# Query, output and transpose matmuls reordered within a turn, and a layer-norm chain of 14 tiles spread over three turns

## The reference

```
x = x + attention(layernorm(x))     # 32 query heads, 8 key/value heads of 64, rotary positions, causal softmax
x = x + experts(layernorm(x))       # 8 experts with 512 hidden channels, the best 2 of them for each token
```

## Time and profile before

| what | us |
|---|---|
| median of three runs | 865.78 |
| the profiled execution | 865.23 |
| span of its profile | 863.3 |
| TensorE busy in the span | 764.6 |
| VectorE busy | 492.0 |
| ScalarE busy | 487.9 |
| GpSimd busy | 459.0 |

### The profile page before, as it was taken

One profiled execution on the slowest core, in us unless ns is written; L12 is line 12 of the kernel. 1 busy time (PEld: TensorE's weight loads), 2 busy tenths in 40 slices (PEclk: granted clock), 3 DMA queues, 4 the chain that ended last, 5 costly groups with the idle time before them and its releaser, 6 DMA issues. The chain is left out here.

```text
span 863.3 us, 18994 instructions
## 1 busy us (share of the span) xinstructions
PE 764.6 (89%) x5895; PEld 640.0 (74%) x5895; DVE 492.0 (57%) x1943; ACT 487.9 (57%) x1537; POOL 459.0 (53%) x690
## 2 busy tenths in 40 slices
PE   3589999999999999999999999936019999999994
PEld 3478888888888888888888888722017888888883
DVE  5777667567576566676666666555962333333331
ACT  1477877777777777777777777825212223222221
POOL 1356565565665665655656556527642445554442
PEclk9799999999999999999999999977559999999998
DMA  6343121211212212212212112038651223333230
GB/s 194 105 126 101 42 56 45 62 50 51 60 45 59 56 36 71 50 39 74 51 38 68 57 38 65 23 115 265 174 190 28 50 44 49 49 52 55 42 56 2
DMA packets 51905, 61.16 MB, mean 71 GB/s; under 512 B 10368, under 2 KB 45440, under 8 KB 51552
## 3 DMA queue, kind: packets, MB, share of 16 engines
q1 hardware_dynamic: 40144, 48.48, 19.6%
q0 software_dynamic: 7488, 9.36, 6.7%
q10 hardware_dynamic: 4176, 2.11, 0.9%
HBM read 26.34 MB, written 9.32 MB: 41 GB/s over the span
## 5 line engine op out<-in xcount | busy, mean ns | idle before, releaser
L794 POOL TENSOR_SCALAR probs<-exps,inv_sums 128x128 f32<-128x128 f32 x256 | 96.0, 375 | 213.8 <-DVE inv_sums L660 159.5
L543 ACT COPY pT<-probsT 128x384 f32<-128x384 f32 x256 | 122.7, 479 | 77.6 <-PE probsT L424 77.5
L424 PE MATMUL probsT<-tables,probs 128*128 128x128 f32 x768 | 132.5, 282 | 8.9 <-POOL probs L795 7.4
L534 ACT ACTIVATE exps<-masked,neg_max 128x128 f32<-128x128 f32 x256 | 103.2, 403 | 46.7 <-DVE neg_max L654 46.0
L536 ACT ACTIVATE exps<-masked,neg_max 128x256 f32<-128x256 f32 x256 | 127.4, 498 | 0.0
L795 POOL TENSOR_SCALAR probs<-exps,inv_sums 128x256 f32<-128x256 f32 x256 | 124.8, 487 | 0.0
L1387 POOL DMA_INDIRECT out<-y,to_token x39 | 61.9, 1587 | 101.8 <-DVE y L1356 79.5
L652 DVE CUSTOM_DVE_ANT_0 masked<-scores,tables 128x128 f32<-128x128 f32 x256 | 71.8, 281 | 76.8 <-PE scores L411 64.1
L424 PEld LDWEIGHTS probsT<-tables,probs 128*128 128x128 f32 x768 | 84.1, 141 | 32.7 <-POOL probs L795 17.2
L654 DVE CUSTOM_DVE_ANT_0 masked<-scores,tables 128x256 f32<-128x256 f32 x256 | 107.4, 419 | 0.0
L411 PE MATMUL scores<-kT,qT 64*128 64x128 f32 (+1 forms) x1024 | 102.8, 341 | 3.9 <-DMA qT<-rotated 3.9
(11 more groups left out here) (150 smaller groups left out, 1818.3 us busy)
## 6 DMA issues: line engine op xcount, KB each, us to landing
qT<-rotated SPq DMA_DIRECT2D x256, 64.0 KB, 2.2
kT<-k_cos SPq DMA_DIRECT2D x64, 128.0 KB, 3.4
experts_w_out<-w_in SPq DMA_DIRECT2D x16, 512.0 KB, 4.5
raw<-w_attn SPq DMA_DIRECT2D x20, 256.0 KB, 3.0
experts_w_out<-w_out SPq DMA_DIRECT2D x2, 2048.0 KB, 10.0
out<-x_all SPq DMA_DIRECT2D x8, 256.0 KB, 2.3
xn_rows<-experts_w_out ACTq DMA_DIRECT2D x4, 512.0 KB, 5.1
x_all<-x SPq DMA_DIRECT2D x1, 1792.0 KB, 10.7
```

Source lines behind the costliest of these rows:

```text
L424: mm = nc.tensor.transpose(p_bank[:, at:at + P], probs[:, h, at:at + P], ident)
L534: nc.scalar.activation(exps[:, h, 0:P], masked[:, h, 0:P], ACT.Exp, bias=neg_max[:, h, 0:1], scale=-1.0, accum_out=sums[:, h, 0:1])
L543: nc.scalar.copy(pT[:, n % 2, h, :], p_bank[:, 0:3 * P]).then_inc(pT_done, 1)
L794: nc.gpsimd.tensor_scalar(probs[:, h, 0:P], exps[:, h, 0:P], inv_sums[:, h, 0:1], 1.0, ALU.mult, ALU.mult)
```

## The change

TensorE's `project_q`, `next_q` and `output` take a first and a last matmul, so that their 12 matmuls can be issued in parts. The transposes of a turn become T1, T2 and T3 of group n-1 and T0 of group n: T1 comes one turn later than before. In a turn without another projection the order is T1, 8 query matmuls, T2, 4 query and 4 output matmuls, T3, 8 output matmuls, T0. In a turn with another projection (the variable `whole`; the x transposes in g = 3 count as one) it is T1, 12 query matmuls, T2, 12 output matmuls, T3, the other projection, T0. ScalarE's copies follow. The chain of 14 tiles is cut: its first part comes at the end of turn 0 on VectorE, two Newton steps come at the end of turn 1, and two in turn 2, ahead of `normalise(1)`.

```diff
 # TensorE
-        def project_q(b, g):
+        def project_q(b, g, first=0, end=12):
...
+            parts = ((xT_hi, w_hi), (xT_lo, w_hi), (xT_hi, w_lo))
+            for i in range(first, end):
+                a, k, (x, w) = i // 6, i // 3 % KT, parts[i % 3]
+                at = k * 2 * P + a * P
+                mm = nc.tensor.matmul(x_bank[:, a * SEQ:(a + 1) * SEQ], w[:, piece, at:at + P], x[:, b % 2, k, :],
+                                      start=(i % 6 == 0), stop=(i % 6 == 5))
+            if end == 12:
+                mm.then_inc(q_ps, 1)
...
             if past(b, g, 1):
+                prob_transposes(*back(b, g, 1), 1)
+            whole = projects(b, g)[0] is not None
+            next_q(b, g, 0, 12 if whole else 8)
+            if past(b, g, 1):
                 prob_transposes(*back(b, g, 1), 2)
-            if prepares(b, g):
-                next_q(b, g)
+            if not whole:
+                next_q(b, g, 8, 12)
+            if past(b, g, 2):
+                output(*back(b, g, 2), 0, 12 if whole else 4)
             if past(b, g, 1):
                 prob_transposes(*back(b, g, 1), 3)
-            if past(b, g, 2):
-                output(*back(b, g, 2), 0)
+            if past(b, g, 2) and not whole:
+                output(*back(b, g, 2), 4, 12)
+            other_projection(b, g)
             prob_transposes(b, g, 0)
-            if past(b, g, 2):
-                output(*back(b, g, 2), 1)
-            other_projection(b, g)
-            prob_transposes(b, g, 1)
 # ScalarE
             if past(b, g, 1):
-                copy_probs(*back(b, g, 1), 2)
+                copy_probs(*back(b, g, 1), 1)
             split_in_slot(b, g, 1)
             exponentials(b, g, 1)
             if past(b, g, 1):
+                copy_probs(*back(b, g, 1), 2)
+            split_in_slot(b, g, 2)
+            if past(b, g, 1):
                 copy_probs(*back(b, g, 1), 3)
-            split_in_slot(b, g, 2)
-            copy_probs(b, g, 0)
             exponentials(b, g, 2)
             exponentials(b, g, 3)
-            copy_probs(b, g, 1)
+            copy_probs(b, g, 0)
 # VectorE
             inverses(b, g, 2)
+            if b == 0 and g == 0:
+                moments_start(TT, TILES)
+            if b == 0 and g in (1, 2):
+                newton_steps(TT, TILES, 2 * g - 2, 2 * g)
             if g == 2 and b < LAST:
                 normalise(b + 1)
...
         split_w(4)
-        layernorm_moments(TT, TILES)
         batches(turn)
```

More of the change, by code:

```diff
@@ L326, in weights_split @@
                 pe.wait_ge(w_split, piece + 1)
-        def project_q(b, g):
+        def project_q(b, g, first=0, end=12):
             piece = PIECES_ATTN.index(("q", g))
[L331 to L336, removed]
+            if first == 0:
+                weights_split(b, piece)
+                if g == 0:
+                    pe.wait_ge(xT_lo_done, b + 1)
+            parts = ((xT_hi, w_hi), (xT_lo, w_hi), (xT_hi, w_lo))
[6 more added lines that the diff above has]
+                mm.then_inc(q_ps, 1)
         def project_k(b, half):
@@ L373, in bank_read, with next_q @@
                 pe.wait_ge(q_parts, turn_of(b, g) + 3)
[L375 to L381, removed]
+        def next_q(b, g, first, end):
+            if not prepares(b, g):
+                return
+            if first == 0:
+                if past(b, g, 1):
+                    bank_read(*back(b, g, 1))
+                else:
+                    pe.wait_ge(q_parts, 2)
+            project_q(*ahead(b, g), first, end)
         def other_projection(b, g):
@@ L450, in values, with output @@
             mm.then_inc(o_ps, 1)
-        def output(b, g, tt):
+        def output(b, g, first=0, end=12):
             piece = PIECES_ATTN.index(("o", g))
-            if tt == 0:
+            if first == 0:
                 weights_split(b, piece)
@@ L461, in output @@
                     pe.wait_ge(y_added, b)
[L462 to L469, removed]
+            parts = ((oT_hi, wo_hi), (oT_lo, wo_hi), (oT_hi, wo_lo))
+            for i in range(first, end):
+                tt, pair, (o, w) = i // 6, i // 3 % PAIRS, parts[i % 3]
+                mm = nc.tensor.matmul(y_bank[:, tt * EMB:(tt + 1) * EMB], o[:, pair, tt * P:(tt + 1) * P],
+                                      w[:, piece, pair * EMB:(pair + 1) * EMB],
+                                      start=(g == 0 and i == 0), stop=(g == KV_HEADS - 1 and i % 6 == 5),
+                                      skip_group_check=True)
+            if g == KV_HEADS - 1 and end == 12:
                 mm.then_inc(y_ps, 1)
@@ L502, in _ @@
         values(LAST, KV_HEADS - 2)
+        prob_transposes(LAST, KV_HEADS - 1, 1)
         prob_transposes(LAST, KV_HEADS - 1, 2)
-        output(LAST, KV_HEADS - 2, 0)
-        output(LAST, KV_HEADS - 2, 1)
+        output(LAST, KV_HEADS - 2)
         prob_transposes(LAST, KV_HEADS - 1, 3)
         values(LAST, KV_HEADS - 1)
-        output(LAST, KV_HEADS - 1, 0)
-        output(LAST, KV_HEADS - 1, 1)
+        output(LAST, KV_HEADS - 1)
     @block.scalar
@@ L591, in _ @@
         out_hi(LAST, KV_HEADS - 2)
+        copy_probs(LAST, KV_HEADS - 1, 1)
         copy_probs(LAST, KV_HEADS - 1, 2)
@@ L721, in turn, with moments_start @@
             inverses(b, g, 2)
+            if b == 0 and g == 0:
+                moments_start(TT, TILES)
+            if b == 0 and g in (1, 2):
+                newton_steps(TT, TILES, 2 * g - 2, 2 * g)
             if g == 2 and b < LAST:
                 normalise(b + 1)
-        def layernorm_moments(a, b):
+        def moments_start(a, b):
             for i in range(a, b):
@@ L734, in layernorm_moments, with newton_steps @@
             wait_own(nc.vector.tensor_scalar(y.bitcast(I32), w.bitcast(I32), -1.0, RSQRT_MAGIC, ALU.mult, ALU.add))
-            for i in range(4):
+        def newton_steps(a, b, first, end):
+            v, y, w = newton[:, 0, a:b], newton[:, 1, a:b], newton[:, 2, a:b]
+            for i in range(first, end):
                 wait_own(nc.vector.tensor_tensor(w, y, y, ALU.mult))
@@ L744, in _ @@
         wait_own(ins)
-        layernorm_moments(0, TT)
+        moments_start(0, TT)
+        newton_steps(0, TT, 0, 4)
         normalise(0, True)
```

## The result

The changed kernel took 856.88 us in the median of 6 runs (854.13 to 859.08), beside 865.84 for the kernel before (6 runs, 865.48 to 869.12). The ratio is 0.9886, with a 95% interval of 0.9862 to 0.9909. It was run again beside 17 runs of the kernel before: 856.47 (5 runs, 853.80 to 856.86) to 866.44, a ratio of 0.9885 (0.9864 to 0.9906). So it is 1.15% or 10 us faster, between 8 and 12. The forecast was 12.5 less, 853.3 us.

What follows compares the result with a forecast made beforehand. The prediction took TensorE's turns as the bound, with waits on the one transpose bank's loop. Steady turns 9.1 plus batch 0 3.4 gave 12.5 us off 865.23, so 852.7, named 853.3; likeliest 850.5 to 856, full range 849.5 to 860.

Steps and rivals of the forecast that it cites:

- What bounds the turn: Steady turns: one PSUM bank's loop of transposes, copy and handovers, 1.15 to 1.18 us, makes TensorE wait 0.11 to 0.14 twice.
- The change doesn't do what it says: Rival, chance 0.07: the 0.24 before T0 is a cost of going from output matmuls to transposes; 864.7 us.
- Turns without another projection: Turns with no key, value or x work: both waits go, 7.57 to 7.26 us, 0.3 less each.
- no spare: Rival, chance 0.08: T2's copy comes 0.2 later than reckoned, turns without another projection gain only 0.1; 857.7 us.
- Turns with keys or values: Turns that also project keys or values: one wait goes and the next block starts earlier, 0.18 us less each.
- The x turn: Turn with the x transposes: the 1.18 us loop binds, scores at 8.16 and not 7.85, a loss of 0.3.
- Steady sum: Batches 1 to 7 together: 9.1 us less, 7.9 of it in batches 1 to 6.
- Slower by ScalarE's loop over turns: Rival, chance 0.06: T3's copy over 0.85 late starts ScalarE late every turn; 868.8 us at 0.25 over.
- Batch 0, turn 0: First turn: 4.5 us of chain leave the path, first maximum near 27.8; gain 3.3, between 2.7 and 4.5.
- Later turns of batch 0: After turn 0: turn 1 gains 0.5, turns 2 and 3 lose 0.5 each, turn 4 loses 0.4, turn 5 gains 0.5.
- Turns 6 and 7 of batch 0: Last two turns of the first batch: a gain of 0.5 us together.
- The start gives all back: Rival, chance 0.17: Newton pieces block with GpSimd and later exponentials hold turns 1 to 4, batch 0 nets 0; 856.7 us.

## Why the prediction was right, and where it was off

The time lies in the stated range, and the mechanism of the steady turns was right. In the start-up the total came out near by terms that were off in both directions, and that is in part luck.

- *What bounds the turn.* Right. The loop of transposes, copy and handovers through one bank was the wait: T3 and T0 now start 0.12 after the matmul ahead, and the shorter copies alone take the old order to the same turn lengths. "The change doesn't do what it says" falls with it.
- *Turns without another projection.* 7.26 forecast, 7.27 or 7.28 measured, and 7.57 before. T2, T3 and T0 at 4.31, 5.59 and 6.87; measured 4.30, 5.58 and 6.86. The margin ahead of T3 was there ("no spare" falls), and the extra copy shows that it is no bigger.
- *Turns with keys or values.* 8.69 forecast, 8.70 measured. *The x turn*: 8.16 forecast, 8.13 measured, with its wait for the copy. *Last two turns and end*: -0.4 forecast; 7.15 and 17.36 against 7.07 and 17.21, -0.2.
- *Steady sum.* 9.1 forecast, 8.8 and 8.6 measured. Both small terms were rounded up: 0.29 and 0.17 for 0.30 and 0.18.
- *Slower by ScalarE's loop over turns*: not seen. No turn from batch 1 on is late, and with 0.30 more on ScalarE the turns with keys or values grew by 0.03 at most.
- *Batch 0, turn 0.* 3.3 forecast, between 2.7 and 4.5; 4.7 measured between the first profiles, 2.9 between the second ones. The mechanism is right: the first maximum comes at 28.43 and 28.26 (27.8 forecast, 32.27 before), and the next thing late is the transfer of piece 6, ahead of the exponentials of head 1. But the term took the transfer's issue from one profile (27.79) as fixed, and added only 0.3 for the clock. Both move: issue at 27.30 and 28.98, the clock 1.00 and 0.50. The scores of turn 1, 36.6 forecast, came at 35.69 and 38.37.
- *Later turns of batch 0.* Turn 1 gave 0.4 and 0.2, 0.5 forecast. Turn 2 is 10.68 and turn 3 is 8.61 (10.26 and 7.88 before): 1.15 given back in the first pair and 0.8 in the second, 1.0 forecast. Turn 4 gave back nothing (9.14, 9.09 before), 0.4 forecast. Turn 5 gave 1.1, 0.5 forecast.
- *Turns 6 and 7 of batch 0* are the term that had the wrong sign: 0.5 forecast as a gain, and 0.1 and 0.9 lost. What turn 5 saves beyond the forecast, turn 6 pays back when VectorE's split waits for GpSimd's addition. Turn 6 is 9.67 to 9.69 in eight of the nine profiles with the new order and 8.82 in the first one alone; with the old order it is 8.82 to 8.87. The earlier trace rows had shown this wait in turn 2, and the prediction looked for it only at the Newton pieces.
- *The start gives all back.* Its number was met: 856.7 stated, 856.88 and 856.47 measured, which is above the 850.5 to 856 of the likeliest case. Its mechanism wasn't: batch 0 nets 5.0 in the first pair and 2.4 in the second and not 0, and turns 2 to 4 give back 1.2 and 0.9. In the medians the chain is worth 0.8 us beside the new order (857.24 to 856.47) and by the ratios 1.9, within what they can tell from nothing, and 0.2 to 3.6 alone.
- *The sum.* 12.5 forecast, 9.0 in the first comparison and 10.0 in the second. The spans of the first profiles differ by 11.1: 8.8 steady and 5.0 in batch 0, less 0.5 for scores that began later and 2.2 behind attention. Those of the second profiles differ by 10.4: 8.6, 2.4 (3.4 forecast) and 0.3 for scores that began earlier, less 0.8 behind attention. So the first profile of the changed kernel was lucky twice, in turn 0 and in turn 6, and unlucky behind attention. I summed against one profile, and behind attention it was the shortest (293.4), where the other 13 profiles have 0.5 to 2.6 more. Which kind the runs without a profile were isn't known, so what the medians lack can't be shared out further.

## What to carry to other kernels

A busy engine can hide waits of a tenth of a microsecond: read the distance of two starts where two kinds of work meet, and look whose copy ended 0.14 us earlier. A bank that two engines hand back and forth sets a shortest distance between its users, and other work must be spread to at least that, in every variant of the turn; the variant that was left out (the x turn) cost 0.42 a time. A wait that is taken away at a start-up is worth only what the next one leaves, so move that one too: here the earlier transfer alone gave nothing, the chain 0.8 us beside the new order, and both together 4.3 (857.24 to 852.95; 1.9 and 5.6 by the ratios). A turn that gets shorter can hand a late instruction on to the next, so add up neighbours: turns 5 and 6 together gained 0.3 in the second pair of profiles, and turn 5 alone 1.1. And take two profiles of each kernel and sort them by what differs in their start before any term is read off.

## What the runs showed of the hardware that I had not expected

Newton's small steps were 0.17 us each where they stood before. Beside GpSimd they were longer, on VectorE and then on GpSimd in the changed kernel's turn 2:

```profile
54.38 0.63 DVE L760 TENSOR_TENSOR newton<-newton 128x14 f32<-128x14 f32 x1
55.05 0.31 DVE L761 TENSOR_TENSOR newton<-newton 128x14 f32<-128x14 f32 x1
55.39 0.43 DVE L762 TENSOR_SCALAR newton<-newton 128x14 f32<-128x14 f32 x1
55.86 0.17 DVE L763 TENSOR_TENSOR newton<-newton 128x14 f32<-128x14 f32 x1
```

```profile
53.31 1.67 POOL L804 TENSOR_TENSOR rotated<-by_cos,by_sin 128x512 f32<-128x512 f32 x1 [0.21 <-DVE by_sin L647]
54.97 0.38 POOL L818 TENSOR_SCALAR probs<-exps,inv_sums 128x128 f32<-128x128 f32 x1
55.31 0.48 POOL L819 TENSOR_SCALAR probs<-exps,inv_sums 128x256 f32<-128x256 f32 x1
```

The first three ended 0.01 to 0.03 after a GpSimd instruction did (54.98, 55.35, 55.79), 0.86 us more for the three. So VectorE waits for whole instructions of GpSimd, as the earlier trace rows showed for a split, and GpSimd for VectorE's (the addition of 1.80 and not 1.29 at the end of turn 5). The Trainium skill says in "SBUF — State Buffer", section "SBUF: two separate sides", that a VectorE instruction with two SBUF inputs, or in a mode that uses two ports, and one of GpSimd that reads SBUF block each other for the whole instruction. These rows agree. The third step has one tensor input and was held too; in which mode it ran no run here shows.

The runs of the changed kernel lay 5.0 and 3.1 apart (854.1 to 859.1, 853.8 to 856.9), those of the kernel before 3.6 and 5.7 (865.5 to 869.1, 864.0 to 869.7). One transfer issued 3 to 5 us earlier brought the five runs of that kernel within 0.6. The same instructions in the same kernel took one of two courses in two places: TensorE's projection ahead of turn 0 stepped by 0.12 or by 0.21, and of two instructions that opened 0.03 apart either VectorE's or GpSimd's went first. The time of a start-up that hangs on these is no constant that one profile can give.
